# Shared expert and combine of a vision-tower kernel on pairs of blocks instead of single blocks

## The reference

```
xf = layernorm(h)                                             # 32 x 257 tokens x 256
shared = silu(xf @ shared_w1.T) * (xf @ shared_w2.T) @ shared_w3.T      # hidden width 1024
scores = sigmoid(xf @ router_w.T);  gates = scores * top2_mask(scores + expert_bias)
h12 = einsum('td,ehd->teh', xf, w12);  h1, h2 = split(h12, 2)
routed = einsum('teh,edh->td', silu(h1) * h2 * gates[:, :, None], w3)   # 8 experts of width 256
out = h + shared + routed
```

## Time and profile before

| | |
|---|---|
| runs | 3029.67, 3040.48, 3041.18 us; median 3040.48 |
| profiled execution | span 3047.3 us from its first to its last instruction, the only time that the page gives for it |
| TensorE busy | 2721.9 us, 89% of the span |
| VectorE, ScalarE, GpSimd busy | 1740.6 us, 1119.3 us, 461.3 us |
| last stage | 2453.8 to 3047.3 us, 593.5 us |
| in it: TensorE, VectorE, ScalarE busy | 582.3 us, 304.3 us, 178.6 us |

### The profile page before, as it was taken

The page is one execution under the profiler, slowest core; times in us unless marked ns, Lnnn a source line. Parts: engine busy times, 40 slices in busy tenths (PEclk is TensorE's granted clock), DMA queues, the critical chain, the costliest instruction groups (busy, mean ns, idle before and its releaser), DMA issues. The chain is left out here.

```text
span 3047.3 us, 57522 instructions
## 1 busy us (share of the span) xinstructions
PE 2721.9 (89%) x16999; PEld 2235.8 (73%) x17000; DVE 1740.6 (57%) x4704; ACT 1119.3 (37%) x2993; POOL 461.3 (15%) x485
## 2 busy tenths in 40 slices
PE   2799999999999999999999456759999989999999
PEld 2677777777777677777776345647777789999999
DVE  6456666666566665666664388853433435555555
ACT  0244444444444444444445121124444423333332
POOL 0010010101010100001010376620000012222222
PEclk9789999999999999999998555579999999999999
DMA  1000000000000000000000153322222211221211
GB/s 52 4 8 12 15 13 12 13 12 12 13 12 12 13 12 13 12 15 13 12 9 12 61 166 116 115 78 83 86 86 84 85 54 55 65 59 55 65 59 53
DMA packets 85246, 131.19 MB, mean 43 GB/s; under 512 B 13314, under 2 KB 59316, under 8 KB 84916
## 3 DMA queue, kind: packets, MB, share of 16 engines
q1 hardware_dynamic: 71988, 93.01, 10.0%
q0 software_dynamic: 13056, 35.67, 3.6%
HBM read 74.07 MB, written 54.03 MB: 42 GB/s over the span
## 5 line engine op out<-in xcount | busy, mean ns | idle before, releaser
L717 DVE TENSOR_REDUCE mx<-ps 128x1 f32<-128x257 f32 x1024 | 395.7, 417 | 326.2 <-PE ps L368 310.4
L564 ACT ACTIVATE pT<-ps 128x257 f32<-128x257 f32 x1024 | 344.3, 383 | 346.3 <-PE ps L385 344.8
L368 PE MATMUL ps<-km,q 128*128 128x258 f32 x1024 | 354.4, 362 | 44.7 <-DVE mx L717 22.4
L368 PEld LDWEIGHTS ps<-km,q 128*128 128x128 f32 x1024 | 202.4, 198 | 139.3 <-issue 59.9
L385 PE MATMUL ps<-q,km 128*128 128x258 f32 x1024 | 288.4, 308 | 1.9 <-ACT pT L564 1.2
L385 PEld LDWEIGHTS ps<-q,km 128*128 128x128 f32 x1024 | 196.3, 197 | 45.5 <-issue 28.8
L890 POOL TENSOR_TENSOR rs<-rs,mhalf 128x2 f32<-128x2 f32 x32 | 22.3, 697 | 1340.3 <-DVE rs L669 1340.3
L1519 PE MATMUL ps<-zhi,whi 128*128 128x256 f32 x1056 | 214.5, 285 | 1.5 <-DVE zlo L1587 1.5
L1519 PE MATMUL ps<-zhi,wlo 128*128 128x256 f32 x1056 | 211.3, 281 | 0.0
L1519 PE MATMUL ps<-zlo,whi 128*128 128x256 f32 x1056 | 210.9, 281 | 0.0
L1592 DVE TENSOR_TENSOR uu<-ps,sil 128x512 f32<-128x512 f32 x132 | 91.2, 691 | 186.1 <-ACT sil L1559 186.1
(11 more groups left out here) (307 smaller groups left out, 6263.2 us busy)
## 6 DMA issues: line engine op xcount, KB each, us to landing
z<-zs SPq DMA_DIRECT2D x140, 128.0 KB, 2.0
ys<-z SPq DMA_DIRECT2D x140, 128.0 KB, 1.8
hb<-hscr SPq DMA_DIRECT2D x66, 256.0 KB, 2.7
hscr<-h SPq DMA_DIRECT2D x34, 256.0 KB, 2.0
xs<-in_x SPq DMA_DIRECT2D x32, 256.0 KB, 3.5
out<-acc SPq DMA_DIRECT2D x32, 256.0 KB, 2.2
uu<-in_wu SPq DMA_DIRECT2D x6, 768.0 KB, 5.1
raw<-in_wu SPq DMA_DIRECT2D x6, 768.0 KB, 5.1
```

Source lines behind the costliest of these rows:

```text
L368: pe.matmul(ps[:, n % 2, 0:NP], q2[p % 2][:, h // 2, t * P:(t + 1) * P], km[p % 2][:, h // 2, h % 2, :], start=True, stop=True).then_inc(m ...
L564: act.activation(pT[:, n // LT, n % LT, :], ps[:, 4 + n % 2, 0:N], ACT.Exp, scale=HD ** -0.5).then_inc(s_ok, 1)
L717: dve.tensor_reduce(mx[:, t, h:h + 1], ps[:, n % 2, 0:N], AX_X, ALU.max, negate=True).then_inc(mx_ok, 1)
```

## The change

The last stage leaves `stage_b` and becomes `shared_and_combine`, with tiles of its own. The weights `whi`, `wlo` and the lists `idxs`, `gates` are allocated around both. `stage_b` is else the same. In the new stage the 33 blocks are 16 **pairs** j of 512 tokens and one single block at the end (`blocks_of(j)` is 2 for j < 16 and then 1). Each pair has NC = 8 steps cu of 128 hidden columns (HALF = 2, K = 33, NPAIR = 16):

- `hidden(j, p, cu)`: 2 matrices times 6 products of 512 columns, so 12 products; w1's result fills bank 2(cu%2), w2's the next one.
- `output(j, cu)`: 4 tiles of 128 tokens times 3 products of 256 columns, so 12 products, into banks 4 and 5.
- `silu`, `product`, `head`, `split`: 128x512, as before, but each from or to one bank.
- `turn`, `z_high`, `z_low`: once a pair at cu = 4, with 8 transposes and instructions of 128x1024.
- `norm_pair`: once a pair, behind the split of cu = 2, 4 instructions of 128x256.
- `combine(j-1)` and `pick(j)`: once a pair, behind the split of cu = 0, with one add of 128x1024 and 8 instructions of 128x256. The copy of the gates moves into `pick`, which now also waits for the end of `combine`.
- The SP queue: one load of 512 KB, and two stores of 256 KB, for each pair.
- GpSimd: 8 indirect DMAs in a row for each pair.

In the single block every one of the 8 steps has 12 products of 256 columns in `hidden`, 6 in `output`, and 128x256 on ScalarE and VectorE.

```diff
-            stage_b(nc, ctx, sem, a, out, hscr, mv3, rs3, eye, ps)
...
+            with ExitStack() as inner:
+                ys = stage_b(nc, inner, sem, a, hscr, mv3, rs3, eye, ps, whi, wlo, idxs, gates)
+            with ExitStack() as inner:
+                shared_and_combine(nc, inner, sem, out, hscr, mv3, rs3, eye, ps, ys, whi, wlo, idxs, gates)
...
+            def load(j, p):
+                nb = blocks_of(j)
+                sp.dma_start(hbp[p][:, 0:nb * LT, :].rearrange("p (n t) d -> p n (t d)", n=nb),
+                             hscr[bass.ds(PAIR * j, nb)].rearrange("n p t d -> p n (t d)")).then_inc(hb3_in[p], 16)
...
+            def pair(j, p):
+                if more(j, 2):
+                    sp.wait_ge(acc_ok, j * AN + 1)
+                    load(j + 2, p)
+                sp.wait_ge(acc_ok, j * AN + AN)
...
+            def hidden(j, p, cu):
+                u, c = cu // HALF, cu % HALF
+                w = blocks_of(j) * L
...
+                if cu >= 2 or later(j):
+                    pe.wait_ge(uu_ok, j * NC + cu - 1)
+                for m in range(2):
+                    mm = [(w_, z_, f) for w_, z_ in ((whi, zph[p]), (wlo, zph[p]), (whi, zpl[p])) for f in range(FT)]
+                    for n, (w_, z_, f) in enumerate(mm):
+                        at = f * 2 * UH + m * UH + c * P
+                        last = pe.matmul(ps[:, 2 * (cu % 2) + m, 0:w], w_[:, u, at:at + P], z_[:, f, 0:w],
+                                         start=(n == 0), stop=(n == len(mm) - 1))
...
+            def output(j, cu):
+
+                u, c = cu // HALF, cu % HALF
+                pe.wait_ge(hhi_ok, j * NC + cu + 1)
+                pe.wait_ge(hlo_ok, j * NC + cu + 1)
+                if cu == 0 and later(j):
+                    pe.wait_ge(acc_ok, j * AN - AN + 1)
...
+            def pair(j, p):
+                for cu in range(NC):
+                    hidden(j, p, cu)
+                    if cu >= 1:
+                        output(j, cu - 1)
+                    elif later(j):
+                        output(j - 1, NC - 1)
+                    if cu == 4 and more(j):
+                        turn(j + 1)
...
+            def pick(j):
+
+                w = blocks_of(j) * LT * TOP
+                if later(j):
+                    dve.wait_ge(y_in, 16 * T * TOP * j)
+                    dve.wait_ge(seen3, j)
+                    dve.wait_ge(acc_ok, AN * j)
+                dve.tensor_copy(gatep[:, 0:w], gates[:, bass.ds(j * T * TOP, w)])
+                dve.tensor_copy(idxp[:, 0:w], idxs[:, bass.ds(j * T * TOP, w)]).then_inc(idx3_ok, 1)
+
+            def combine(j, p):
+
+                nb = blocks_of(j)
+                dve.wait_ge(out_ps, j * NC + NC)
+                if later(j):
+                    dve.wait_ge(out_d, 16 * PAIR * j)
+                dve.tensor_tensor(accp[:, 0:nb * LT, :].rearrange("p (b t) d -> p b (t d)", b=nb), ps[:, 4:4 + nb, :],
+                                  hbp[p][:, 0:nb * LT, :].rearrange("p (b t) d -> p b (t d)", b=nb),
+                                  ALU.add).then_inc(acc_ok, 1)
+                dve.wait_ge(y_in, 16 * TOP * LT * (PAIR * j + nb))
                 for c in range(TOP):
-                    dve.wait_ge(acc_ok, k * AN + c + 1)
...
+                    dve.wait_ge(acc_ok, j * AN + c + 1)
+                    for n in range(nb):
+                        for t in range(LT):
+                            at = n * LT * TOP + c * LT + t
+                            last = dve.scalar_tensor_tensor(out=accp[:, n * LT + t, :], in0=yg[:, n * LT + t, c, :],
+                                                            scalar=gatep[:, at:at + 1], in1=accp[:, n * LT + t, :],
+                                                            op0=ALU.mult, op1=ALU.add)
                     last.then_inc(acc_ok, 1)
...
+            def pair(j, p):
+                for cu in range(NC):
+                    product(j, cu)
+                    split(j, cu)
+                    if cu == 0 and later(j):
+                        combine(j - 1, 1 - p)
+                        pick(j)
+                    if cu == 2 and more(j):
+                        norm_pair(j + 1, 1 - p)
+                    if cu == 4 and more(j):
+                        z_low(j + 1, 1 - p)
```

More of the change, by code:

```diff
@@ L1467, in stage_b, with later @@
     idx3_ok, y_in, seen3 = sem("idx3_ok"), sem("y_in"), sem("seen3")
-    AN = 1 + TOP
-    yg = raw2[:, 0:LT * TOP * D].rearrange("p (t c d) -> p t c d", t=LT, c=TOP)
-    with nc.Block() as block:
[L1471 to L1477, removed]
+    def later(j):
+        return not isinstance(j, int) or j > 0
@@ new lines, in blocks_of, with more, pairs @@
+    def blocks_of(j):
+        return PAIR if not isinstance(j, int) or j < NPAIR else 1
+    def more(j, m=1):
+        return not isinstance(j, int) or j + m <= NPAIR
+    with nc.Block() as block:
+        def pairs(eng, pair, ahead=0):
+            rounds = (NPAIR - 2 - ahead) // 2
+            pair(0, 0)
+            with eng.Fori(0, rounds) as i:
+                pair(2 * i + 1, 1)
+                pair(2 * i + 2, 0)
+            for j in range(2 * rounds + 1, NPAIR + 1):
+                pair(j, j % 2)
@@ L1492, in _ @@
-            blocks3(sp, step)
-            sp.dma_start(out[:, 0, :], acc[0:B, 0, :]).then_inc(out_d, 16)
+                load(p, p)
+            pairs(sp, pair, 2)
+            sp.dma_start(out[:, 0, :], accp[0:B, 0, :]).then_inc(out_d, 16)
             sp.wait_ge(out_d, 16 * K)
@@ L1523, in output @@
[L1523 to L1535, removed]
-                last.then_inc(out_ps, 1)
@@ L1538, in blk @@
[L1538 to L1547, removed]
+            def hidden(j, p, cu):
+                u, c = cu // HALF, cu % HALF
+                w = blocks_of(j) * L
+                if cu == 0:
+                    pe.wait_ge(hi3_ok, j + 1)
+                    pe.wait_ge(lo3_ok, j + 1)
+                if cu >= 2 or later(j):
[6 more added lines that the diff above has]
+                                         start=(n == 0), stop=(n == len(mm) - 1))
+                last.then_inc(hid_ps, 1)
@@ L1568, in z_high, with silu @@
[L1568 to L1578, removed]
+            def silu(j, cu):
+                w = blocks_of(j) * L
+                act.wait_ge(hid_ps, j * NC + cu + 1)
+                if cu >= 2 or later(j):
+                    act.wait_ge(uu_ok, j * NC + cu - 1)
+                act.activation(silp[:, cu % 2, 0:w], ps[:, 2 * (cu % 2), 0:w], ACT.Silu).then_inc(sil_ok, 1)
@@ L1624, in blk @@
-            def blk(k, p):
-                nxt = not isinstance(k, int) or k < K - 1
-                for u in range(NS):
-                    product(k, u)
-                    split(k, u)
-                    if u == 0 and later(k):
-                        gather(k - 1, 1 - p)
-                        pick(k)
-                    if u == 1 and nxt:
-                        dve.wait_ge(hb3_in[1 - p], 8 * (k + p) + 16)
-                        norm(dve, k + 1, hb[1 - p], z3[0], z_ok3)
-                    if u == 2 and nxt:
-                        z_low(k + 1, 1 - p)
@@ L1640, in _, with pair @@
+            def pair(j, p):
+                for cu in range(NC):
+                    product(j, cu)
[5 more added lines that the diff above has]
+                        norm_pair(j + 1, 1 - p)
+                    if cu == 4 and more(j):
+                        z_low(j + 1, 1 - p)
+            norm_pair(0, 0)
             pick(0)
             z_low(0, 0)
-            blocks3(dve, blk)
```

195 lines of the change are left out of this document (106 added, 89 removed).

## The result

The changed kernel takes **3059.34 us** (median of four runs, 3055.11 to 3063.51), the kernel before 3040.67 beside it (four, 3029.67 to 3041.18). The ratio is 1.0069, with a 95% interval of 1.0044 to 1.0093: slower by 0.7%. 3064 was predicted.

A forecast was written before the change was run, and what follows sets the result against it. TensorE's sum of products was taken to bound the stage. Terms -6.3 + 24.6 + 3.3 + 3.7 - 1.7 = +23.6 us on a median of 3040.5 gave 3064 us, 0.8% slower, range 3047 to 3083 with chance 0.72.

The forecast's parts named there:

- The stand: Each pair from 1 to 15: TensorE waits at output of step 1 for VectorE's `hlo`; 1.64 us each, +24.6 us.
- the late add: Output of step 0: add ready at 4.13 plus 0.15, wanted at 4.23; said to be swallowed by the larger wait.
- The products: TensorE in 16 pairs: a 512-column product takes 232.5 ns against 236.6 for two of 256; -6.3 us (-10 to -2.5).
- outputs as many as before and as wide: nothing: Output products, 96 in a pair, unchanged in number and width, were claimed to change the time by nothing.
- The start: Start of the last stage, where nothing hides the larger load, norms, transposes and `z_high`/`z_low`: +3.7 us (2.5 to 5.5).
- The tail after the last `hidden`: End of the stage: last chain on 256 columns saves 1.0 us, six fewer outputs 0.72; -1.7 us.
- The single block: Last block: the previous pair's combine makes `hlo` of step 1 late; 2.14 us steps just in time; +3.3 us (2.3 to 4.5).
- Costed at nothing: Within a pair: `z_high`, `z_low`, four norms, the load, SP's order, GpSimd's fetches and the new allocation, claimed to cost nothing.
- GpSimd's 8 fetches take about 10 us of 36: GpSimd in each pair: its eight fetches fit in the pair's time, so they were put at no cost.
- That wide products are cheaper than in the routed experts: Rival: 512-column products cost less than 232.5 ns; under 225 the whole is within 0.5%; at 213, 3044 us; chance 0.12.
- That the clock falls in each stand: Rival: after each TensorE wait the first `hidden`s run at half clock, 2.6 us fifteen times, +39, 3103 us; chance 0.07.
- The 512 KB load: Rival: a pair's load is late for the norms; landing at 12 us costs 2.5 in 14 pairs, +35, 3099; chance 0.04.

The follow-up runs named there:

- spread_gap: The changed kernel with the combine cut up over several steps and a pair's fetches in two series of four: 3029.0 us, ratio 0.9967 to the kernel before.
- spread: The changed kernel with the combine cut up over steps 0, 1 and 3, fetches still eight in a row: 3049.9 us, ratio 1.0029 to the kernel before.
- narrow: The changed kernel with each product of 512 columns made as two of 256: 3082.42 us, ratio 1.0151 to the kernel before.

## Why the prediction was right, and where it wasn't

**The stand.** It came where the working put it, with the releaser that it named, in the 15 pairs that it named. The steps agree one by one. Counted from the end of `hidden` of step 0 (2740.80), the add starts at 2.91 and takes 1.22, the multiply-adds start at 4.16, and the pick at 7.67, all as written. The multiply-adds come at 0.41 us and not at 0.43, and the pick waits 0.13 behind them. Only its copies are slower, 0.11 us each, so `uup` starts at 7.89 instead of 7.81 and the output at 10.11 instead of 10.03. The 1.53 us of idle time mustn't be compared with the 1.57 of the working: it starts at the modelled end of the last product, and the working counts from start to start. By starts, `hidden` of step 2 and the stand take 4.44 us (2746.47 to 2750.91) where `hidden` of step 0 takes 2.75 (2738.05 to 2740.80), so the stand is 1.69. With the slower first products behind it, and the rest of the pair the same, the price is the changed kernel's pair less that of spread_gap: 35.90 - 34.10 = 1.80 us, not 1.64. Fifteen times: +27.0, not +24.6.

One reading failed beside it: the late add was not swallowed. The first product of the output of step 0 takes 0.23 us in place of 0.12 (2744.98 to 2745.21), and the last one ahead of it 0.05 more, 0.15 in a pair. Spread_gap has the same (and the same 4.1 us of waits for `accp`), so it isn't in the 1.80 but in the 34.10.

**The products.** This is the term that was mis-sized. The price of a wide product was right, 229 ns against 232.5, and its gain over two narrow ones a little less than written (-3.7 us, not -6.3). But "outputs as many as before and as wide: nothing" was wrong: products of an unchanged width got 2 to 5 ns cheaper, 0.72 us in a pair, -11.5 us. Together -15.4 us, outside of the bounds of -10 to -2.5 that I drew from one row of another stage. These 15.4 are net of the late add's 0.15 in a pair. -15.4 + 27.0 is the +11.6 of the ledger. The estimate by the Trainium skill (TensorE: Matmul & The Clock Gate, section on the back-to-back issue gap), 2.5 ns for each wide product and so 3.8 us, happens to meet the width's own gain of 3.7; its level of 109.2 ns for 256 columns is still not reached by the 113 of the best rows.

**Single block, start, end.** The start was right (+3.4 against +3.7). The tail after the last `hidden` is 1.8 us shorter (1.7 was written). The single block costs 5.0, not 3.3. Its stand is 2.79 us, released by `hpl` like the others, as worked out. Two things were missing. Of 5.8 us of outputs in a block before, 1.44 ran beside the last chain; now only 0.72 do, and the pair's own last output of 1.44 comes ahead, so at the old prices TensorE has 17.1 us of products before the last chain, not 15.7. And steps of 2.14 that are "just in time" were 0.1 to 0.2 late in most of the rest.

**Costed at nothing.** Norms, `z_high` and `z_low`, loads and the order on SP cost nothing indeed. "GpSimd's 8 fetches take about 10 us of 36" is true of its time and was too easily said of its effect: near the end of a series, increments come up to 2.6 us late in spread and once 3.1 in narrow. In the changed kernel silus are 1.1 to 1.3 us late in 14 pairs, at steps with room, so they cost nothing there. Between spread and spread_gap lie 22 us (603.0 and 580.9); how much of that is the pause's and how much the chip's isn't known.

**The number.** That 3064 came within 5 us of 3059.34 is in part luck. The products came out 9.1 us lower than written, the stands 2.4 and the single block 1.7 higher.

**The rivals.** That wide products are cheaper than in the routed experts was true by 3.5 ns only: at 229 ns they aren't under the 225 that the rival asked for. The products as a whole did get 15.4 us cheaper, but for another reason, and the stand outweighs it. That the clock falls in each stand did not happen, but it was closer than its 0.07 says: with 0.38 us more of standing it falls in most pairs, and the stage is 44 us longer than before instead of 18. The 512 KB load landed in 3.6 us and was never late.

## What to carry to other kernels

Doubling the tile of a stage that TensorE bounds also doubles what other engines do behind one step, while the steps stay as long. What counts is not an engine's total but its longest run of work between two results that TensorE waits for, against the room in the steps there: 0.85 us here. Spread such work over the steps before making the tile larger; done so, with the fetches in two series, the same pairs were faster than the single blocks, 0.9967.

## What the runs showed of the hardware that I had not expected

- **The clock's cliff.** After a stand of 1.53 us TensorE went on at 2.4 GHz in 15 of 15 pairs. After 1.91 us it fell to 1.2 GHz in 12 of 15, up to 1.3 us after work had begun again, and cost another 1.6 us. A stand just short of that looks harmless in the profile.
- **An instruction's wait costs more than its idle time.** The pick's wait showed as 0.13 us of idle VectorE and was worth 0.3 us: without a wait, one starts up to 0.1 us before the end of the one ahead.
- **Late increments.** In five traces silus started over 1 us, once 3.1 us, after TensorE's last product near the end of a series of eight indirect fetches, with TensorE's semaphore record as late as the silu. In nine others none did, among them three with series of eight, and in one of these with the same timing. Four of the five are the four traces of one chip, so the condition is not known, and neither is whether the kernel has a part in it.
- **Products of the same width at two prices**: 256 columns every 118 to 120 ns in the old order, every 113 to 118 in the new, at the same granted clock of 1.00.
